# First attention of a two-layer vision tower: the value projection moves ahead of the scores, and VectorE's two Horner sums come to stand on either side of the keep mask

## The reference, cut to what matters

```python
qkv = x @ Wqkv + bqkv                       # 8 heads of 64
scores = einsum('bhnd,bhmd->bhnm', q, k) * SCALE
top_val = top_k(scores, 64)[0][..., -1:]    # 64 of the 65 keys are kept
scores = where(scores < top_val, -inf, scores)
attn = softmax(scores)
v_curr, res = v, 0
for i in range(3):                          # three powers of attn
    v_curr = attn @ v_curr
    res = res + alphas[i] * v_curr
out = res @ Wout + bout
```

## Time and profile before

| | us |
|---|---|
| three runs | 1721.77, 1724.46, 1727.43 |
| median | 1724.46 |
| span of the profiled execution | 1699.7 |
| patch embedding and first layer norm | to about 303 |
| first attention | about 303 to 803 |
| first mixture, second attention, second mixture | from about 803 |
| TensorE busy, share of the span | 95% |
| VectorE, ScalarE, POOL busy | 64%, 51%, 46% |
| TensorE's mean granted clock | 0.981 of full speed |

### The profile page before, as it was taken

The page is one execution under the profiler, slowest core; times in us unless marked ns, Lnnn a source line. Parts: engine busy times, 40 slices in busy tenths (PEclk is TensorE's granted clock), DMA queues, the critical chain, the costliest instruction groups (busy, mean ns, idle before and its releaser), DMA issues. The chain is left out here.

```text
span 1699.7 us, 61682 instructions
## 1 busy us (share of the span) xinstructions
PE 1616.2 (95%) x24097; PEld 1203.3 (71%) x24097; DVE 1082.2 (64%) x3361; ACT 869.2 (51%) x2334; POOL 782.4 (46%) x932
## 2 busy tenths in 40 slices
PE   8999999899999999997989998999999999869997
PEld 3444444677877777776567755888888888659997
DVE  0000005688888888885676664577777777768875
ACT  0000004666666666663544445566766666547753
POOL 0000000588888888886001111445555555645554
PEclk9999999999999999999989999999999999969999
DMA  9887860000000000000400000000000000135431
GB/s 366 338 309 301 321 244 1 2 4 4 3 3 3 3 3 3 3 3 4 111 1 1 1 1 5 3 8 22 22 21 21 21 24 18 36 102 154 141 80 44
DMA packets 47214, 117.17 MB, mean 69 GB/s; under 512 B 10731, under 2 KB 29470, under 8 KB 46972
## 3 DMA queue, kind: packets, MB, share of 16 engines
q1 hardware_dynamic: 39198, 99.25, 16.4%
q0 software_dynamic: 6096, 12.94, 2.2%
q10 hardware_dynamic: 1678, 1.43, 0.3%
HBM read 96.80 MB, written 18.61 MB: 68 GB/s over the span
## 5 line engine op out<-in xcount | busy, mean ns | idle before, releaser
L1545 PE MATMUL ps<-xn,s_a_wqkv 128*128 128x260 f32 x1024 | 276.9, 402 | 4.5 <-DMA s_a_wqkv<-in_f_b 2.9
L201 PE MATMUL ps<-x_chunk,s_w_tok 128*128 128x512 f32 x576 | 252.1, 599 | 6.5 <-DMA x_chunk<-in_x_main 6.5
L201 PEld LDWEIGHTS ps<-x_chunk,s_w_tok 128*128 128x128 f32 x576 | 109.9, 192 | 147.4 <-issue 147.4
L1545 PEld LDWEIGHTS ps<-xn,s_a_wqkv 128*128 128x128 f32 x1024 | 177.0, 191 | 50.2 <-issue 16.3
L228 DVE SCALAR_TENSOR_TENSOR h<-ps,s_b_tok,s_pos 128x512 f32 (+1 forms) x16 | 11.3, 746 | 248.8 <-PE ps L209 248.8
L886 POOL TENSOR_TENSOR prob_a<-e_a,inv_sum_a 128x512 f32<-128x512 f32 x64 | 66.9, 1045 | 194.4 <-issue 113.4
L2161 POOL DMA_INDIRECT out<-h,xn x93 | 97.6, 1049 | 89.6 <-DVE h L2276 85.1
L1629 PE MATMUL ps<-s_a_wqkv,xn_pair_a 128*64 128x256 f32 x1024 | 138.8, 391 | 0.0
L941 ACT ACTIVATE resT_a<-ps 128x260 f32<-128x260 f32 x256 | 85.2, 386 | 101.4 <-PE ps L1596 64.6
L1411 DVE TENSOR_REDUCE neg_max_a<-ps 128x8 f32<-128x520 f32 x128 | 89.2, 697 | 70.8 <-PE ps L1519 48.5
L870 POOL TENSOR_TENSOR kept_a<-e_a,keep_a 128x585 f32<-128x585 f32 x64 | 87.2, 1362 | 71.0 <-issue 60.4
(11 more groups left out here) (280 smaller groups left out, 4265.6 us busy)
## 6 DMA issues: line engine op xcount, KB each, us to landing
x_chunk<-in_x_main SPq DMA_DIRECT2D x96, 768.0 KB, 8.8
xn<-pair_rows SPq DMA_DIRECT2D x93, 130.0 KB, 2.1
pair_rows<-pad_rows_m SPq DMA_DIRECT2D x29, 130.0 KB
s_f_all<-in_f_w SPq DMA_DIRECT2D x2, 1024.0 KB
x_ends<-in_x_tail SPq DMA_DIRECT2D x16, 96.0 KB, 10.8
out<-h,xn POOLq DMA_INDIRECT x93
s_w_tok<-in_w_tok SPq DMA_DIRECT2D x6, 192.0 KB, 8.2
pair_rows<-rows_m,slot_i_m POOLq DMA_INDIRECT x65, 2.5
```

The costliest lines, as they stand in the source:

```text
L201: last = nc.tensor.matmul(ps[:, bank, :], w_tok[:, k, :], xb[:, s, k, :], start=(k == 0), stop=False)
L1545: nc.tensor.matmul(ps[:, QK_BANK[i], 0:QUAD], w_qkv[:, c * P:(c + 1) * P], xn[:, t.h * QUAD:(t.h + 1) * QUAD], start=True, stop=True).then ...
```

## The change

TensorE: `project_v(t)` is issued as the first thing of a step instead of after the scores, and `products(t)` follow `scores(t)`. VectorE: `order_out(t, 0)` is issued before the keep mask instead of after it. `order_out(t, 1)` stays where it was. No instruction is added or taken away, no buffer and no wait is changed. The second attention (not masked) and every other stage are as before.

```diff
@@ -1430,6 +1430,7 @@ (VectorE's step)
                             last = nc.vector.max(low8[:, 0, CH, :], cls_score())
                         last.then_inc(low_done, 1)
+                order_out(t, 0)
                 if t.has(2) and masked:
                     upto(dve, low_done, t.s - 1, pairs)
                     last = nc.vector.tensor_tensor(keep[:, :, 0:CH], score(), over_keys(low8[:, :, 0:CH, 1]),
@@ -1438,7 +1439,6 @@
                     last.then_inc(keep_done, 1)
-                order_out(t, 0)
                 order_out(t, 1)
@@ -1815,9 +1815,10 @@ (TensorE)
             def attend(t):
+                if masked:
+                    project_v(t)
                 scores(t)
                 if masked:
-                    project_v(t)
                     products(t)
                     transpose_cls(t)
```

## The result

| | before | after |
|---|---|---|
| median, us | 1724.99 (1721.77 to 1727.43) | 1768.45 (1762.1 to 1772.27) |
| ratio, 95% interval | 1 | 1.0249 [1.0227, 1.0271] |
| span of the profile, us | 1699.7 | 1770.4 |
| 54 full steps of the first attention, us | 409.8 | 441.0 |
| pair of steps, mean, us | 15.18 | 16.33 |

The kernel is slower, as forecast, but by 43.5 us instead of 17: the measured time lies outside of the range from 1724 to 1756.

A forecast was written before the change was run, and what follows sets the result against it. TensorE was taken to bound the first attention. A pair of steps would grow from 15.18 to 15.75 us; 30 x 0.57 = 17 us on the median of 1724.46 gave about 1742 us, range 1724 to 1756.

The forecast's parts named there:

- What bounds the kernel: First attention: TensorE is the bound, busy 403.84 of 409.80 us; about 0.8 us delay a step makes other chains the bound.
- Part 1, TensorE's own order: TensorE's new order of V, scores, products: saves 0.16 us in the odd step, nothing in the even one.
- Part 2: Scores come late relative to products: everything hanging on them moves 1.18 us (odd) or 1.01 us (even) later.
- ScalarE, even step: Exponentials queued ahead of the products' copies make these 0.52 us later, all passed to TensorE; even to odd 8.34 us.
- ScalarE, odd step: V, heading the even step, waits for the fourth key copy; even step's products start 7.28 us after the odd step's.
- VectorE, odd step: Chain from minimum through mask and sum: `probs_out` ends 7.33 us after products start, making odd to even 7.35 us.
- The sum without pauses: Pair of steps in the first attention without pauses: 8.34 + 7.35 = 15.69 us against 14.83, 0.86 more.
- The pauses: TensorE pauses with no shown cause, 0.35 us a mean pair, fall largely beneath the new waits, leaving 0.06.
- third rival: Pauses in the first attention are not covered, or new waits add their own: 27 us, 1751, up to 1758; 22%.
- The ends: Partial pairs at the ends of the first attention: about three more beside 27 full ones, each 0.57 us longer.

The follow-up runs named there:

- e10: Changed kernel with 14 of 16 class-token products a step left out and ScalarE's copies ahead of its exponentials in even steps; ratio 1.0068 to the kernel before.
- e4: Changed kernel with ScalarE copying the last products before its exponentials in even steps; ratio 1.0229 to the kernel before.
- e11: Changed kernel with, in even steps, ScalarE's copies before its exponentials and V between scores and class scores; ratio 1.0102 to the kernel before.
- e8: Changed kernel with 14 of 16 class-token products a step left out; 1740.83 us, ratio 1.0084 to the kernel before.
- e9: Kernel before with 14 of 16 class-token products a step left out; 1712.44 us, ratio 0.9917 to the kernel before.

## Why the prediction was right and wrong

- **What bounds the kernel: right.** TensorE by a small margin, and a delay of some 0.8 us in front of the other chains makes them the bound. They did.
- **Part 1, TensorE's own order: right.** Scores to products cost 0.48 in the odd step (606.26 to 606.74), V to scores 1.05 (611.78 to 612.83), forecast 1.02; entering V from 128x128 tiles costs 0.34 idle (620.79), what entering the scores cost. e10 shows the gain of 0.16 where nothing covers it, 7.83 instead of 7.98. The Trainium skill's drain at a change of tiling mode (TensorEngine Tiling, Key Properties) agrees with the idle 0.34 and 0.38 in these rows. But a change has no fixed price: in the same pair only 0.07 us stand between scores and class scores and 0.09 between class scores and products.
- **Part 2: right.** The minimum begins at P+0.29 (607.03) and P+0.13 (614.18); forecast 0.30 and 0.14.
- **ScalarE, even step: right in mechanism, covered in fact.** Exponentials at P+2.02, forecast P+2.02; copies at P+2.61, forecast P+2.71; TensorE idle 0.73 in this pair, forecast 0.8. But that is the rare even step: in the median one the copies begin at P+2.90, in the kernel after as in e4, since a pause has made the products' own end as late.
- **ScalarE, odd step: right, and it decides.** V at P+5.04 (611.78), forecast P+5.05; products at P+7.31, forecast P+7.28. Two errors cancel in it: the key copies end at 609.75 + 1.81 = P+4.82, not P+4.99, and V starts 0.22 after their end, not 0.06. e11 confirms the cause.
- **VectorE, odd step: forecast 0.36 too late.** `probs_out` ends at 613.04 + 0.67 = P+6.97; I had P+7.33. The Horner sum starts 2.41 us after the minimum, not 2.53, since unlike the mask it does not wait for MAX8's last result; and the sum to `probs_out` took 0.85, not 1.01. It made no difference to this kernel; ScalarE's P+7.28 was the other term.
- **The sum without pauses: 15.69 forecast, 7.30 + 8.23 = 15.53 measured.**
- **The pauses: this is the step that failed.** I wrote that "these now fall largely beneath the new waits" and let 0.35 us a pair shrink to 0.06. They did not fall beneath the waits, and they grew: 16.33 - 15.53 = 0.80 us a pair, half of it in even steps (8.63 - 8.23), half in odd ones (7.70 - 7.30), where the three pauses behind the products make 5 of the 11 us. In even steps it went the other way round: ScalarE's delay fell beneath the pauses, which 24 of 27 had. The difference of 0.74 is 27 x 0.74 = 20 us of the 26 that the forecast missed (of 38.9 - 17.1 = 22 by the two profiles). I had taken the pauses as a given quantity with no cause, when their place (nearly always inside the densest run of small instructions: 5.6 us of the kernel before at L1596, 1.0 at L1545) was a clue that the change would act on them: it took away the one slow stretch between two dense runs. The third rival came nearest, and it too only let them stay as they were.
- **The ends: too small.** I allowed three pairs at 0.57, 1.7 us. The parts of the stage outside of the 27 full pairs grew from 481.9 - 409.3 = 72.6 to 520.8 - 440.9 = 79.9 us, by 7.3; e8 against e9 has the same 7.0 (74.3 and 67.3), so it does not depend on the instruction supply. Which step of the ramp pays stays open.

Together, 17.1 + 20 + 5.6 less the 0.16 x 27 = 4.3 of the smaller sum gives 38.4, against 38.9 in the two profiles. The medians differ by 43.5 with an interval of 4 us either way, so the other 4.6 us cannot be told from noise.

## What to carry to other kernels

Ask of every slow, sparse instruction that is moved what it separated. V's one microsecond was useless to the matmuls, but two things lived on it: the other engines' lead (scores well before the products that share their queues) and the fetch of an unrolled program. In a step whose engines have little room (here some 0.8 us in 7.6), work out each chain against the event with which it shares a queue, and carry its lateness into the next step: a shift that eats the slack turns hidden waits into the bound at once. And a pause with no named cause is a term with a place: look at the instruction packets before calling it a constant.

## What the runs showed of the hardware that was not expected

- TensorE starves on instructions at full clock. Pieces are 16 KB, their packets take about 1.1 us, and every pause over 0.45 us inside the products of the first attention ended 1.19 to 1.60 us after a packet landed, in all profiles. The longest in the kernel after lasted 2.1 us.
- Fewer instructions can save more than their own time: 14 one-column matmuls a step left out saved 13 us in one order and 28 in the other, though a pair without pauses became no shorter in the first (14.83 us).
- Two executions of one program differed by 30 us in span (1699.7 and 1729.7), 19 of them in the second attention; the cause is open, and no run here tells it.
